# All 71 expert slots add their second bias on TensorE; GpSimd's 47 additions to the records go

## The reference

```python
x = _layernorm(x + attn(x))
for i in range(n_exp):
    wi = wf[:, i:i + 1]
    h = relu(xf * wi @ w1[i] + b1[i])
    y = h @ w2[i] + b2[i]
    out = where(wi > 0, y, out)
x = _layernorm(x + out)
```

## Time and profile before

| what | us |
|---|---|
| median of 3 runs (444.86 to 447.8) | 447.26 |
| the profiled execution, its own time | 446.81 |
| its span in the trace | 445.0 |

### The profile page before, as it was taken

How to read it: one execution, slowest core, us unless ns; L and a number is a source line. 1 busy time by engine, 2 the same in 40 slices (tenths; PEclk the granted TensorE clock), 3 DMA queues, 4 the chain that set the end, 5 groups by cost and what they waited for, 6 DMA issues and landing times.

```text
span 445.0 us, 10570 instructions
## 1 busy us (share of the span) xinstructions
PE 395.4 (89%) x2806; PEld 311.5 (70%) x2806; DVE 368.7 (83%) x1216; ACT 344.2 (77%) x980; POOL 325.1 (73%) x299
## 2 busy tenths in 40 slices
PE   5998899899998887999999994979997999999983
PEld 3654555555555554567878783868997999999983
DVE  6479999999999998857889987686885788788784
ACT  2676999999998898988899883775874777767762
POOL 2067899999999997957027666567672788888866
PEclk9999999999999999999999997796998999999998
DMA  7165766665766544160001154464664878867800
GB/s 222 32 146 142 178 155 152 158 148 133 171 145 149 133 119 118 40 198 2 1 14 63 61 170 140 136 176 143 193 204 133 253 224 227 226 186 214 226 32 27
DMA packets 44378, 62.20 MB, mean 140 GB/s; under 512 B 6670, under 2 KB 29713, under 8 KB 42400
## 3 DMA queue, kind: packets, MB, share of 16 engines
q1 hardware_dynamic: 39712, 52.20, 45.2%
q0 software_dynamic: 4320, 8.93, 5.4%
q10 hardware_dynamic: 288, 0.41, 0.3%
HBM read 47.99 MB, written 13.97 MB: 139 GB/s over the span
## 4 chain that ended last, share of the span: by engine, by line
PE 36%; POOL 30%; issue 13%; DMA 8%; DVE 6%; ACT 5%; POOLq 0%; ACTq 0%; DVEq 0%; SPq 0%
POOL states L2637 13%; PE bank L761 10%; PE bank L745 9%; DMA expert_regions<-row_buffers,row_i 6%; PE bank L371 4%; PE bank L395 3%; POOL o_scale L2649 3%; POOL x_sb L2655 3%; POOL expert_regions L596 3%; POOL out_rows L942 3%; POOL row_buffers L2628 3%; POOL slab L2643 2%; PE bank L1129 2%; PE bank L408 1%; DVE h2t L909 1%
## 5 line engine op out<-in xcount | busy, mean ns | idle before, releaser
L596 POOL DMA_INDIRECT expert_regions<-row_buffers,row_i x64 | 61.6, 962 | 46.3 <-ACT row_buffers L461 25.2
L942 POOL DMA_INDIRECT out_rows<-h2t x71 | 70.4, 992 | 23.3 <-issue 14.2
L761 PE MATMUL bank<-ew,h2t 128*128 x568 | 78.7, 283 | 6.5 <-DVE h2t L893 6.4
L745 PE MATMUL bank<-h2t,slab 128*128 128x128 f32 x568 | 79.8, 286 | 0.5 <-ACT h2t L779 0.5
L761 PEld LDWEIGHTS bank<-ew,h2t 128*128 128x128 f32 x568 | 71.3, 197 | 8.7 <-issue 8.5
L2637 POOL TENSOR_TENSOR states<-states,queries 128x1024 f32<-128x1024 f32 x32 | 75.2, 2373 | 2.8 <-DVE states L2232 2.8
L745 PEld LDWEIGHTS bank<-h2t,slab 128*128 128x128 f32 x568 | 72.5, 200 | 1.7 <-issue 1.0
L2232 DVE TENSOR_TENSOR_SCAN states<-bank,kv 128x512 f32<-128x512 f32 x64 | 72.9, 1203 | 0.3 <-ACT bank L1583 0.2
L884 DVE TENSOR_SCALAR h2t<-bank,slab 128x128 f32<-128x128 f32 x142 | 43.0, 348 | 6.8 <-PE bank L745 6.4
L786 ACT ACTIVATE h2t<-bank,slab 128x128 f32<-128x128 f32 x142 | 43.8, 362 | 5.4 <-PE bank L745 3.4
L779 ACT ACTIVATE h2t<-bank 128x128 f32<-128x128 f32 x71 | 19.6, 276 | 30.7 <-PE bank L751 29.9
(11 more groups left out here) (216 smaller groups left out, 897.8 us busy)
## 6 DMA issues: line engine op xcount, KB each, us to landing
slab<-in_slabs SPq DMA_DIRECT2D x71, 258.0 KB
kv<-values_by_head SPq DMA_DIRECT2D x30, 512.0 KB, 5.6
h2t<-expert_regions SPq DMA_DIRECT2D x71, 72.0 KB, 3.1
x_sb<-in_x SPq DMA_DIRECT2D x32, 128.0 KB, 6.0
values_by_head<-row_buffers SPq DMA_DIRECT2D x15, 256.0 KB, 2.1
out_rows<-h2t POOLq DMA_INDIRECT x71
expert_regions<-row_buffers,row_i POOLq DMA_INDIRECT x64, 2.3
expert_regions<-pad_record SPq DMA_DIRECT2D x9, 72.0 KB, 3.1
```

The source lines that it names most:

```text
L596: pool.indirect_dma_start(out=regions, out_offset=bass.IndirectOffsetOnAxis(ap=row_i[:, q, g:g + 1].bitcast(U32), axis=0), in_=rec[:, ring ...
L745: ins = pe.matmul(to[:, at:at + P], slab[:, item % SLABS_C, c * P:(c + 1) * P], c_xwt[:, s, :], start=True, stop=True)
L761: ins = pe.matmul(bank[7][:, 0:D], c_ht[:, s, c * P:(c + 1) * P], ew2[:, bass.ds(e * HC + c * D, D)], start=(c == 0), stop=(c == HC - 1 an ...
L942: pool.indirect_dma_start(out=out, out_offset=bass.IndirectOffsetOnAxis(ap=rc[:, q, D + 1:D + 2].bitcast(U32), axis=0), in_=c_y[:, item % ...
```

## The change

`BIAS_FROM`, `x_biased`, `bias_rows_in` and POOL's register reads go. `back` gives every slot the fifth product. The order of everything else on every engine stays as it was; in POOL's order only the 47 calls of `bias_rows_in` are taken out.

```diff
-BIAS_FROM = EARLY
...
-                biased = item < BIAS_FROM
                 for c in range(HC):
-                    ins = pe.matmul(bank[7][:, 0:D], c_ht[:, s, c * P:(c + 1) * P],
-                                    ew2[:, bass.ds(e * HC + c * D, D)], start=(c == 0), stop=(c == HC - 1 and not biased))
-                if biased:
-                    ins = pe.matmul(bank[7][:, 0:D], three[:, :], bias_rows[:, bass.ds(e, D)], start=False, stop=True)
-                ins.then_inc(y2_done, 1)
+                    pe.matmul(bank[7][:, 0:D], c_ht[:, s, c * P:(c + 1) * P],
+                                    ew2[:, bass.ds(e * HC + c * D, D)], start=(c == 0), stop=False)
+                pe.matmul(bank[7][:, 0:D], three[:, :], bias_rows[:, bass.ds(e, D)], start=False,
+                          stop=True).then_inc(y2_done, 1)
...
                 dve.wait_ge(y2_done, item + 1)
-                if item >= BIAS_FROM:
-                    dve.wait_ge(x_biased, item - BIAS_FROM + 1)
                 dve.tensor_tensor(c_z[:, z, :], bank[7][:, 0:D], rc[:, item % RECORDS_C, 0:D],
...
-            def bias_rows_in(item):
...
-                pool.tensor_tensor(rows, rows, eb2[:, bass.ds(known[item], D)], ALU.add).then_inc(x_biased, 1)
-
...
             scatter(5, 6, 7)
             scatter(5, 7, 8)
-            bias_rows_in(24)
-            bias_rows_in(25)
-            bias_rows_in(26)
             store(12)
             store(13)
             store(14)
-            bias_rows_in(27)
-            bias_rows_in(28)
-            bias_rows_in(29)
             store(15)
...
-            bias_rows_in(69)
-            bias_rows_in(70)
             store(67)
             store(68)
             store(69)
             store(70)
```

More of the change, by code:

```diff
@@ L642, in gla_moe @@
         xw_done, xwt_done, xwt_evac, h_done = (sem(n) for n in ("xw_done", "xwt_done", "xwt_evac", "h_done"))
-        relu_act, relu_dve, y2_done, z_added, c_stats, c_rstd, yn_ready, x_biased = (
-            sem(n) for n in ("relu_by_act", "relu_by_dve", "y2_done", "z_added", "c_stats", "c_rstd", "rows_normed",
-                             "x_biased"))
+        relu_act, relu_dve, y2_done, z_added, c_stats, c_rstd, yn_ready = (
+            sem(n) for n in ("relu_by_act", "relu_by_dve", "y2_done", "z_added", "c_stats", "c_rstd", "rows_normed"))
         dve_c = Chain(sem("dve_c_chain"), 1)
@@ L919, in phase_c_pool @@
         def phase_c_pool(pool):
-            known = {}
-            def bias_rows_in(item):
[L923 to L933, removed]
-                pool.tensor_tensor(rows, rows, eb2[:, bass.ds(known[item], D)], ALU.add).then_inc(x_biased, 1)
             def store(item):
@@ L944, in store @@
                     in_=c_y[:, item % ROWS_C, :], in_offset=None, bounds_check=NTOK - 1, oob_is_err=False).then_inc(out_sc[item % 8], 16)
-            return bias_rows_in, store
+            return store
         block = ctx.enter_context(nc.Block(no_gpsimd_drain=True))
@@ L2689, in _ @@
             scatter = phase_b_pool(pool)
-            bias_rows_in, store = phase_c_pool(pool)
+            store = phase_c_pool(pool)
             apply_q(13, 0)
@@ L2788, in _ @@
             store(14)
-            bias_rows_in(27)
-            bias_rows_in(28)
-            bias_rows_in(29)
             store(15)
-            bias_rows_in(30)
             store(16)
             store(17)
-            bias_rows_in(31)
             store(18)
             store(19)
-            bias_rows_in(32)
-            bias_rows_in(33)
             store(20)
@@ L2803, in _ @@
             store(22)
-            bias_rows_in(34)
             store(23)
-            bias_rows_in(35)
-            bias_rows_in(36)
             store(24)
-            bias_rows_in(37)
             store(25)
             store(26)
-            bias_rows_in(38)
             store(27)
             store(28)
-            bias_rows_in(39)
-            bias_rows_in(40)
             store(29)
-            bias_rows_in(41)
-            bias_rows_in(42)
             store(30)
             store(31)
-            bias_rows_in(43)
             store(32)
-            bias_rows_in(44)
             store(33)
@@ L2830, in _ @@
             store(38)
-            bias_rows_in(45)
-            bias_rows_in(46)
             store(39)
-            bias_rows_in(47)
-            bias_rows_in(48)
             store(40)
-            bias_rows_in(49)
             store(41)
-            bias_rows_in(50)
-            bias_rows_in(51)
             store(42)
             store(43)
-            bias_rows_in(52)
             store(44)
             store(45)
-            bias_rows_in(53)
-            bias_rows_in(54)
             store(46)
             store(47)
-            bias_rows_in(55)
             store(48)
-            bias_rows_in(56)
-            bias_rows_in(57)
             store(49)
@@ L2856, in _ @@
             store(51)
-            bias_rows_in(58)
             store(52)
-            bias_rows_in(59)
-            bias_rows_in(60)
             store(53)
@@ L2865, in _ @@
             store(57)
-            bias_rows_in(61)
             store(58)
[L2868 to L2871, removed]
             store(59)
             store(60)
-            bias_rows_in(66)
             store(61)
             store(62)
-            bias_rows_in(67)
             store(63)
             store(64)
-            bias_rows_in(68)
             store(65)
             store(66)
-            bias_rows_in(69)
-            bias_rows_in(70)
             store(67)
```

## The result

Over 20 runs each, the changed kernel takes 448.31 us (446.38 to 450.88) and the kernel before 447.39 (444.86 to 449.35). The ratio is 1.0032, with a 95% interval of 1.0017 to 1.0048: slower by 0.9 us between the medians and by 1.4 by the ratio, inside the 1% that was called no change. The forecast was 0.6 us, 447.9. The profiled execution of the changed kernel took 448.69 us, its span is 446.9.

A forecast was written before the change was run, and what follows sets the result against it. PE was taken to bound the late slots, interrupted by POOL's additions. Slots 24 to 69 grow by 1.15 us, mostly regained: +0.3 at the end, +0.3 for stores, +0.6 in all, median 447.9, range 445.2 to 451.0.

The forecast's parts named there:

- The fifth product costs 4.7 us: PE, 45 late steps: 2.00 us with the fifth product against 1.895 without, 0.105 a step, 4.7 us in all.
- The additions give back 3.6 us: PE's waits in slots 24 to 69, put down to POOL's additions, go with them: 3.6 us, bounds 0 and 3.6.
- Slot 24 to 69 in 90.0 us: PE from `back` of slot 24 to slot 69: 45 steps of 2.00, 90.0 us in place of 88.85.
- The end: +0.3 us: POOL's last stores: most of the 1.15 us delay regained, last store at 442.57 in place of 442.25.
- Stores that move up: +0.3 us: POOL's stores from slot 12 run earlier, beside slot 24's record load, for which PE waits: 0 to 0.7 us, taken as 0.3.
- The sum: Whole kernel: +0.3 at the end and +0.3 for the stores, +0.6 us, median 447.9.
- DVE in bank 7's loop: Rival: DVE becomes late between `back` and next `back`, PE waits; 2.8 us more, 450.7; chance 0.12.
- Waits that stay: Rival: POOL's DMA issues, not its additions, slow DVE; PE's waits remain, 3.6 us more, 451.5; chance 0.06.
- The nearly hidden product: Rival: the fifth product on PE costs only 0.06 a step, 2.0 us lower, 445.9; chance 0.10.

The follow-up runs named there:

- The two timings: Changed kernel with POOL's stores from slot 12 held until slot 26's records are weighed, timed twice: 1.0003 and 1.0023 to before; changed kernel 1.0032 and 1.0037.
- the stores held: Changed kernel, POOL waiting for the records of slot 26 ahead of the store of slot 12: 447.94 us, and 448.26 us when run again.

## Why the prediction held, step by step

- *The fifth product costs 4.7 us.* Measured 4.90. Right, and the row that was chosen, a step of 2.00 without a wait, is the one that came out. The rival price, the passage of 0.055 alone, is one half of it; the other half shows only when an fp32 product follows (2.00 first or last in `back`, 1.95 to 1.96 ahead of a transpose). It lies in the fp32 group right behind the product, 1.11 us in place of 1.06; that it is the next fp32 weights' load, which cannot hide behind so short a product, fits all three, but was not shown by itself.
- *The additions give back 3.6 us.* Measured 3.64. Longer steps alone would have taken 1.39 of it; 2.25 stay with them. The reason given, that the additions are queued between stores, was right but not sharp: in another order the same additions cost 0.6. That the first ones made the rest late, since they held the stores back until slot 24's records and the next had landed, fits POOL's timeline but was not shown apart from the rest of the order.
- *Slot 24 to 69 in 90.0 us.* 90.11.
- *The end: +0.3 us.* Here a term was mis-sized. I put slot 67's store 0.3 us behind its `norm_out`, the pause between two stores of a busy POOL; a store that finds POOL waiting started 0.86 behind it. That `norm_out` came earlier than forecast, 0.73 us after `back` of slot 69 (438.30 to 439.03) and not 0.99. So the last store started 5.80 us after `back` of slot 69, where 442.57 - 437.03 = 5.54 was forecast. (The bound that did not count, 442.35, is 442.34 by its own terms.) With 0.11 more in the 45 steps, it is 95.91 us from `back` of slot 24 to the last store against 95.22 before: +0.7 in place of +0.3.
- *Stores that move up: +0.3 us*, between 0 and 0.7. The mechanism is seen, but on slot 26's records (3.13 us) and not on slot 24's: 2.07, where 2.4 to 3.1 was forecast. The two timings say 1.3 and 0.6, with overlapping intervals, the entries at a like clock 0.7 and 0.3. The term may have been too small; its size stays open. No term had the entry's own spread: 0.84 between two profiles of the kernel before, the clock at 1.00 in one and down in the other.
- *The sum.* 0.7 and 0.3 to 1.3 make 1.0 to 2.0; measured 0.9 between the medians and 1.4 by the ratio, whose interval, 0.8 to 2.1, leaves the forecast of 0.6 just outside. The sign and the reason were right, since the two large terms, 4.90 and 3.64, came out as forecast; what was short lies at the two ends of the stretch.
- *The rivals.* DVE in bank 7's loop: no wait of PE for L887 from slot 25 to 69. Waits that stay: none. The nearly hidden product: only in another order, at 0.065.

The Trainium skill, "TensorE: Matmul & The Clock Gate", section "Back-to-back issue gap", has 56 ns for the matmul by itself. The trace agrees for its passage (349.08 to 349.13, and 0.05 to 0.06 elsewhere). The section calls that figure too low for a stream that also loads weights, for which it has about 81 ns; the step here pays 109.

## What to carry to other kernels

When an in-order queue is late for another engine, look for the first instruction in it that waits long, and at what ready work stands behind it: another order on POOL, with seven ready stores ahead of the first addition and one addition behind each later store, gained 3.3 us, while taking all additions away for a product on the bounding engine lost 0.9 to 1.4. Moving work onto the engine that sets the pace costs its full price, so price it by a whole step of the pipeline with the work in it, not by the distance to the next instruction. POOL's delay behind the instruction that it waited for was longer than its pause between two stores (0.86 against 0.3 us), and at the end of this kernel it was the former that counted. The entry differed by 0.84 us between two profiles of the unchanged kernel before, so compare two profiles from a common point on, and look at the clock there.

## What the runs showed of the hardware

- A bf16 product over 3 partitions, between products over 128, cost 0.25 us a step more than the same product over 128 (2.25 against 2.00): neither its weights nor the next ones were loaded ahead.
- What the short bf16 product cost depended on its successor: 0.109 us a step ahead of fp32 products, 0.065 ahead of a transpose.
- The granted clock after the pause at slot 24 differs from run to run of one kernel: 1.00 after 2.43 us of idle time and 0.50 after 4.42 in the changed kernel; 1.00 after 2.27 and 0.50 after 3.25 with the stores held.
- DVE's `norm_out` was slowed by POOL's additions: 0.61 beside two of them and 2.04 for two beside four, against 0.35 alone. In the changed kernel, where POOL only stores, no single one from 352 us to 436 took more than 0.35.
